# A convolution with fused attention and layer norm: the 7x7 convolution from two column tiles with 49 taps to four with 48 relative taps, and work moved between the engines

## What is computed

```python
k = conv(x, w1, dilation=2, padding=6) + b1
k = conv1x1(k, w2) + b2                       # 49 logits per pixel
attn = softmax(k, axis=1)
y = einsum('bkchw,bkhw->bchw', shifts(x), attn)
yc = states @ Cmat                            # states: scan s = A s + Bvec over the width
out = y + gelu(yc.T + y * D)
out = layernorm_over_channels(out) * ln_w + ln_b
```

## Time and profile before

| | us |
|---|---|
| median of 3 runs | 952.96 (952.06 to 953.69) |
| the profiled execution | 954.34 |
| its span | 952.2 |
| PE busy | 897.1, 94% |
| PEld busy | 762.8, 80% |
| DVE busy | 705.8, 74% |
| ACT busy | 418.9, 44% |
| POOL busy | 128.3, 13% |
| mean granted clock of PE | 0.977 |

### The profile page before, as it was taken

One profiled execution on the slowest core, in us unless ns is written; L12 is line 12 of the kernel. 1 busy time (PEld: TensorE's weight loads), 2 busy tenths in 40 slices (PEclk: granted clock), 3 DMA queues, 4 the chain that ended last, 5 costly groups with the idle time before them and its releaser, 6 DMA issues.

```text
span 952.2 us, 29640 instructions
## 1 busy us (share of the span) xinstructions
PE 897.1 (94%) x13764; PEld 762.8 (80%) x13764; DVE 705.8 (74%) x904; ACT 418.9 (44%) x499; POOL 128.3 (13%) x104
## 2 busy tenths in 40 slices
PE   4979889999999999999999999999999999999585
PEld 4979788877888788877888788878888788878572
DVE  0489957877878778877878877876978777875356
ACT  1134514435444544436444544435444543444436
POOL 1785000012100200012000200013000200012010
PEclk9979999999999999999999999999999999999779
DMA  9250050002340026002420027002520022002204
GB/s 299 63 89 3 1 91 2 3 1 46 64 73 3 1 46 134 3 1 45 85 53 2 1 46 135 2 2 45 104 34 2 2 47 45 2 2 46 45 2 88
DMA packets 133634, 41.92 MB, mean 44 GB/s; under 512 B 133175, under 2 KB 133256, under 8 KB 133256
## 3 DMA queue, kind: packets, MB, share of 16 engines
q1 hardware_dynamic: 132248, 40.01, 20.2%
q10 hardware_dynamic: 1264, 0.04, 0.1%
HBM read 23.27 MB, written 16.78 MB: 42 GB/s over the span
## 4 chain that ended last, share of the span: by engine, by line
PE 71%; DVE 10%; ACT 4%; issue 3%; DVEq 0%; ACTq 0%
PE cv L389 39%; PE wk L440 11%; PE wk L423 9%; PE wk L474 4%; PE ms L454 3%; PE ms L461 3%; DVE V L958 2%; ACT AT L660 2%; DVE o L1105 1%; DVE R L870 1%; PE ms L402 1%; ACT V L626 1%; DVE st L1046 1%; DVE chs L1048 1%; DVE st L1052 1%
## 5 line engine op out<-in xcount | busy, mean ns | idle before, releaser
L389 PE MATMUL cv<-V,W 128*49 128x248 f16 (+3 forms) x9408 | 545.0, 271 | 8.5 <-DVE V L958 4.3
L389 PEld LDWEIGHTS cv<-V,W 128*49 128x49 f16 x9408 | 478.1, 105 | 55.1 <-issue 34.7
L626 ACT ACTIVATE V<-R,sc 128x1024 f16<-128x1024 f32 (+1 forms) x88 | 110.7, 1261 | 23.0 <-DVE R L874 11.4
L958 DVE SCALAR_TENSOR_TENSOR V<-R,sc,V 128x1024 f16<-128x1024 f32 (+1 forms) x88 | 114.5, 1303 | 2.8 <-ACT V L626 1.8
L440 PE MATMUL wk<-band,XT 128*128 128x224 f16 (+1 forms) x960 | 110.2, 269 | 3.1 <-DVE o L1085 1.5
L440 PEld LDWEIGHTS wk<-band,XT 128*128 128x128 f16 x960 | 82.6, 99 | 31.3 <-issue 10.2
L267 POOL TENSOR_TENSOR chs<-o 128x1024 f32<-128x1024 f32 x14 | 33.0, 2355 | 497.3 <-DVE o L1085 471.5
L423 PEld LDWEIGHTS wk<-AT,sel 128*128 128x128 f16 x2560 | 80.5, 101 | 16.9 <-issue 10.9
L671 ACT ACTIVATE tg<-tg 128x1024 f32<-128x1024 f32 x32 | 33.8, 1058 | 132.5 <-DVE tg L1075 132.5
L423 PE MATMUL wk<-AT,sel 128*128 128x16 f16 x2560 | 88.8, 192 | 2.5 <-ACT AT L660 2.5
L1075 DVE SCALAR_TENSOR_TENSOR tg<-wk,sc,yc 128x512 f32<-128x512 f32 x64 | 47.7, 747 | 47.5 <-PE wk L440 47.5
(11 more groups left out here) (140 smaller groups left out, 785.7 us busy)
## 6 DMA issues: line engine op xcount, KB each, us to landing
raw<-in_x_dram SPq DMA_DIRECT2D x16, 1024.0 KB, 11.8
out_dram<-o SPq DMA_DIRECT2D x28, 512.0 KB, 4.9
w1raw<-in_L_conv_w_dram SPq DMA_DIRECT2D x2, 3136.0 KB, 17.7
out_dram<-o SPq DMA_DIRECT2D x8, 256.0 KB, 3.4
cm<-in_L_conv_Cmat_dram ACTq DMA_DIRECT2D x1, 32.0 KB, 8.8
dcol<-in_L_conv_D_dram ACTq DMA_DIRECT2D x2, 0.5 KB, 10.0
b2col<-in_L_conv_b_dram ACTq DMA_DIRECT2D x2, 0.2 KB
lnw<-in_L_conv_ln_w_dram ACTq DMA_DIRECT2D x2, 0.5 KB, 6.7
```

Source lines behind the costliest of these rows:

```text
L389: ins = pe.matmul(bank.rearrange("p (t c) -> p t c", c=COLS)[:, :, c0:c1], W[:, wl, h, s * K7 + v, :], V[a % RING][:, xl, w, t0:t0 + WIN, ...
L626: nc.scalar.activation(v_array(a, 0), array(a), ACT.Identity, scale=sc[:, par, 3:4]).then_inc(vhi, 1)
L958: nc.vector.scalar_tensor_tensor(out=v_flat(a, 1), in0=array_flat(a), scalar=sc[:, par, 3:4], in1=v_flat(a, 0), op0=ALU.mult, op1=ALU.subt ...
```

## The change

It keeps the algorithm and its units, and changes how the convolution is laid on PE and who does what.

- The 49th tap is subtracted from the weights of the others at the start (w2 relative to its last row, the bias too), and its logit is 0 (`last_tap`): 48 taps, kept as 32 and 16. `W` has the high and the low part side by side, 96 columns.
- A matmul has 32 or 16 weight columns on a column tile 32 wide (`tile_position`), and its data are both column parities at once (2 x 8 windows x up to 32 columns). Products run in 7 blocks of two (X and Y). Two (half, tap) steps of both are one double step of 20 matmuls, five per tile (`ROUNDS`): 49 double steps and 980 matmuls per unit for 1176.
- A sum is spread over partitions; some taps' parts lie on the fourth tile. ACT copies two of the sums (`sum_1`, `sum_2`), DVE adds the others straight from `cv` (`add_sum`, `fold_in`), now with both parities at once in four banks. `wk` goes from four banks to two; the logits are turned in two halves into it, and `gather_taps` adds the parts.
- The softmax: the shift is the exponential's bias and its sum comes out of `accum_out`, one instruction per 49 logits, 16 per unit.
- c0, c1, c2 and w are made by POOL (semaphore `pool_rows`). The bound on |x| is a sum of absolute values by ACT (`bound`) instead of DVE's maximum. ACT evacuates `apply`'s result (`attended`), and `gelu_args` and `residual` work on whole rows in SBUF.
- The second variance of unit m - 1, its inverse deviation and `normalise` move to the start of the next unit but one. `conv`'s first block of a unit waits for `logits_d` of the unit before it.

The lists of ACT and DVE after, for unit n (items of the next unit marked '):
ACT: v_high 2, 3; inverse_deviation(m-1,1); affines(m-1,1); exponentials 0-7; v_high 4; exponentials 8-15; v_high 5; attention_high; turned_attention; sum_1; band 0; v_high 6; band 1; v_high 7; bands 2, 3; bound' 0; bands 4, 5; bound' 1; band 6; v_high 8; bands 7, 8; v_high 9; band 9; sum_2; v_high 10; attended and gelu (0,0), (0,1), (1,0); v_high' 0; attended and gelu (1,1); squares 0; turned_x 0, 1; inverse_deviation 0; turned_x 2, 3; affines 0; turned_x 4, 5; squares 1; turned_x 6, 7; v_high' 1.
DVE: logits_i, logits_0 of m; v_low 2, 3; gather_taps 0; normalise(m-1,1); gather_taps 1; last_tap; softmax_shift; x2+, x2-; v_low 4; softmax_divide; v_low 5; attention_low; y2+, y2-; v_low 6; band 0; q2; band 1; v_low 7; band 2; q3; band 3; logits_1; band 4; q1; bands 5, 6; v_low 8; bands 7, 8; v_low 9; band 9; logits_2; u1', u0'; v_low 10; gelu_args (0,0); x1+'; residual (0,0); logits_rows; gelu_args (0,1); x1-'; residual (0,1); gelu_args (1,0); scales'; residual (1,0); v_low' 0; gelu_args (1,1); u2'; residual (1,1); centre 0; turned_x 0, 1; normalise 0; turned_x 2, 3; y1+'; turned_x 4, 5; y1-'; centre 1; turned_x 6, 7; v_low' 1; logits_d.

```diff
+REL = TAPS - 1
+TA, TB = 32, 16
...
+ROW_STEPS, POOL_ROWS = 17, 4
...
+M1P, M1M, M2P, M2M, M0, MD, MI = range(7)
+BLOCKS = (((M1P, 0, 0, 0), (M1M, 1, 1, 0)), ((M1P, 2, 2, 0), (M1M, 3, 3, 0)),
+          ((M2P, 4, 4, 0), (M2M, 5, 5, 0)), ((M2P, 6, 6, 0), (M2M, 7, 7, 0)),
+          ((M0, 8, 8, 0), (MD, 8, 9, 0)), ((M0, 9, 10, 1), (MI, 8, 11, 1)), ((M0, 9, 9, 0), (MI, 10, 12, 0)))
+NBLOCKS = len(BLOCKS)
+SUM_FIRST, SUM_LAST = (0, 0, 2, 2, 4, 4, 5), (1, 1, 3, 3, 6, 4, 6)
+BLOCK_ARRAYS = (2, 4, 6, 8, 9, 10, 11)
+BLOCK_SETS = (2, 4, 6, 8, 10, 12, 13)
...
+SLOT_FREE = (-3, -1, 0, 0, 1, 1, 2, 2, 3, 3, 4)
...
+STREAMS = {"A0": (0, 32, 0), "A1": (64, 96, 0), "A2": (0, 32, 1), "B0": (32, 64, 0), "B1": (32, 48, 1)}
...
+ROUNDS = ((X, 0, "A0", 0), (X, 1, "A1", 0), (X, 2, "B0", 0), (X, 3, "A2", 0),
+          (X, 0, "A0", 1), (X, 1, "A1", 1), (X, 2, "B1", 0), (X, 3, "A2", 1),
+          (Y, 0, "A0", 0), (Y, 1, "A1", 0), (X, 2, "B0", 1), (Y, 3, "B0", 0),
+          (Y, 0, "A2", 0), (Y, 1, "A0", 1), (X, 2, "B1", 1), (Y, 3, "B1", 0),
+          (Y, 0, "A1", 1), (Y, 1, "A2", 1), (Y, 2, "B0", 1), (Y, 3, "B1", 1))
...
-        cv = ctx.enter_context(nc.psum_tensor("cv", [P, 2, BANK], F32))
-        wk = ctx.enter_context(nc.psum_tensor("wk", [P, 4, BANK], F32))
+        cv = ctx.enter_context(nc.psum_tensor("cv", [P, 4, BANK], F32))
+        wk = ctx.enter_context(nc.psum_tensor("wk", [P, 2, BANK], F32))
...
+            def difference(buffer, par, j):
+
+                nc.gpsimd.tensor_tensor(R[buffer][:, :, :, :], rows_of(par, j + 2), rows_of(par, j),
+                                        ALU.subtract).then_inc(pool_rows, 1)
+
...
             def unit(n, par, nxt=True):
                 m = n - 1
-                sum_rows(m, 0)
+                make_c2(n, par)
+                make_w(n, par)
                 if nxt:
                     amax(n + 1, 1 - par)
+                    make_c1(n + 1, 1 - par)
+                sum_rows(m, 0)
                 sum_squares(m, 0)
                 sum_rows(m, 1)
                 sum_squares(m, 1)
-                pool.wait_ge(var_done, 2 * n)
+                if nxt:
+                    make_c0(n + 1, 1 - par)
...
+                for d in range(first, last):
+                    b, s = d // DSTEPS, 2 * (d % DSTEPS)
+                    if d % DSTEPS == 0:
+                        pe.wait_ge(vlo, ARRAYS * n + BLOCK_ARRAYS[b])
                         if cold:
+                            pe.wait_ge(w_low, 2 * BLOCK_SETS[b])
+                        if b == 0 and n:
+                            pe.wait_ge(z_step, ZSTEPS * n - 3)
+                        if b == 2 and n:
+                            pe.wait_ge(z_step, ZSTEPS * n)
+                        if b == 4:
+                            pe.wait_ge(z_step, ZSTEPS * n + 3)
+                        if b == 5:
+                            pe.wait_ge(z_step, ZSTEPS * n + 4)
+                    begun, left = set(), {(g, t): ROUNDS_LEFT[g, t] for g in (X, Y) for t in range(4)}
+                    for g, t, kind, later in ROUNDS:
+                        total, a, ws, t0 = BLOCKS[b][g]
+                        k0, k1, low = STREAMS[kind]
+                        h, v = (s + later) % HALVES, V_ORDER[(s + later) // HALVES]
+                        c0, c1 = max(0, PAD - v), min(COLS, COLS + PAD - v)
+                        left[g, t] -= 1
+                        to = cv[TILE * t:TILE * t + k1 - k0, bank_of(n)[total], :]
+                        ins = pe.matmul(to.rearrange("p (w t c) -> p w t c", w=2, c=COLS)[:, :, :, c0:c1],
+                                        W[:, ws, h * K7 + v, k0:k1],
+                                        slot(n, a)[:, low, :, t0:t0 + WIN, h, c0 + v - PAD:c1 + v - PAD],
+                                        skip_group_check=True, tile_position=(0, TILE * t),
+                                        start=(b == SUM_FIRST[total] and s == 0 and (g, t) not in begun),
+                                        stop=(b == SUM_LAST[total] and s == BLOCK_STEPS - 2 and not left[g, t]))
+                        begun.add((g, t))
...
+            def turn_logits(m, w):
+                if w == 0:
+                    pe.wait_ge(z_step, ZSTEPS * m + ZSTEPS)
+                    pe.wait_ge(xt_low, 8 * m + 8)
+                else:
+                    pe.wait_ge(soft, SOFT * m + 2)
+                for t in range(WIN):
+                    ins = pe.transpose(wk[:, t // 4, (t % 4) * P:(t % 4 + 1) * P],
+                                       Z[:, w, t].rearrange("p k c -> p (k c)"), id32[:, :])
+                ins.then_inc(lt_ready, 1)
...
-                if r >= 4:
-                    pe.wait_ge(blo, 10 * m + r - 3)
+                if r >= 2:
+                    pe.wait_ge(blo, 10 * m + r - 1)
...
-                if y >= 4:
-                    pe.wait_ge(o_made, 8 * m + y - 3)
+                if y >= 2:
+                    pe.wait_ge(xs_made, 8 * m + y - 1)
...
             def unit(n, par):
                 m = n - 1
+                conv(n, 0, 1)
+                if m:
+                    variance(m - 1, 1)
+                conv(n, 1, 3)
+                turn_logits(m, 0)
+                conv(n, 3, 5)
+                turn_logits(m, 1)
+                conv(n, 5, 16)
                 turn_attention(m, 0)
                 turn_attention(m, 1)
+                conv(n, 16, 18)
                 for r in range(BROWS):
                     spread(m, r)
+                    conv(n, 18 + r, 19 + r)
                 for y in range(8):
                     apply(m, y)
+                    conv(n, 28 + y, 29 + y)
+                    if y == 6:
                         mean(m, 0)
+                turn_x(n, par, 0)
+                conv(n, 36, 37)
+                turn_x(n, par, 1)
+                conv(n, 37, 39)
+                variance(m, 0)
+                conv(n, 39, 40)
+                for g in range(2, 6):
                     turn_x(n, par, g)
+                    conv(n, 38 + g, 39 + g)
                 mean(m, 1)
+                conv(n, 44, 45)
+                turn_x(n, par, 6)
+                conv(n, 45, 46)
+                turn_x(n, par, 7)
+                conv(n, 46, CONV)
...
+                nc.scalar.activation(tg[:].rearrange("p h r w -> p (h r w)"),
+                                     raw[par][:, h, PAD:PAD + ROWS, :].rearrange("p r w -> p (r w)"), ACT.Abs,
+                                     accum_out=amx[:, par, h:h + 1]).then_inc(amax_part, 1)
...
+            def exponentials(m, first, last):
+                act.wait_ge(soft, SOFT * m + 7)
+                for i in range(first, last):
+                    nc.scalar.activation(E[:, i, :], E[:, i, :], ACT.Exp, bias=st[:, 1, i:i + 1],
+                                         accum_out=st[:, 2, i:i + 1]).then_inc(exp_done, 1)
...
+            def attended(m, par, q, h):
+
+                if q == 0 and h == 0:
+                    act.wait_ge(o_free, 64 * m + 64)
+                for w in range(2):
+                    y = 4 * q + 2 * h + w
+                    act.wait_ge(y_done, 8 * m + y + 1)
+                    nc.scalar.activation(o[:, q, h, :, w:WIDTH:2], wk[:, y % 2, :].rearrange("p (r c) -> p r c", c=COLS),
+                                         ACT.Identity, scale=sc[:, par, applied_scale(m):applied_scale(m) + 1]
+                                         ).then_inc(xs_made, 1)
...
+            def add_sum(n, par, out, s, other, op, steps, p0=0, p1=P, scale=4):
+
+                dve.wait_ge(conv_done, NBLOCKS * n + SUM_LAST[s] + 1)
+                dve.wait_ge(z_step, ZSTEPS * n + steps)
+                nc.vector.scalar_tensor_tensor(out=out, in0=summed(n, s, p0, p1), scalar=sc[0:p1 - p0, par, scale:scale + 1],
+                                               in1=other, op0=ALU.mult, op1=op).then_inc(z_step, 1)
...
+            def gather_taps(m, w):
+
+                dve.wait_ge(lt_ready, 2 * m + w + 1)
+                dst = E[:, w * WIN:(w + 1) * WIN]
+                a = wk[:].rearrange("p b (t e k) -> p (b t) k e", e=P // TA, k=TA)[:, :, :, 0:2]
+                nc.vector.tensor_reduce(dst[:, :, 0:TA], a, AX, ALU.add).then_inc(soft, 1)
+                b = wk[:].rearrange("p b (t e k) -> p (b t) k e", e=P // TB, k=TB)[:, :, :, 4:8]
+                nc.vector.tensor_reduce(dst[:, :, TA:REL], b, AX, ALU.add).then_inc(soft, 1)
```

More of the change, by code:

```diff
@@ L733, in unit @@
                 affines(m, 0)
-                turned_x(n, par, (6, 8))
+                turned_x(n, par, 4, 6)
                 squares(m, 1)
-                products(n, par, 2)
-                inverse_deviation(m, 1)
+                turned_x(n, par, 6, 8)
                 if nxt:
-                    prepare(n + 1, 1 - par)
+                    v_high(n + 1, other, 1)
             def weights_high(first, last):
-                for h, s, src, scale, step in list(weight_parts())[HALVES * first:HALVES * last]:
+                for s in range(first, last):
```

(15 more changed lines are left out.)

901 lines of the change are left out of this document (443 added, 458 removed), and 3 rows, old and new, of the table PRODUCTS.

## The result

The changed kernel takes 978.62 us (median, 976.8 to 986.2) where the kernel before takes 953.17: 1.028 times as long by the means of the runs, 95% interval 1.023 to 1.034. I had said 945, range 925 to 972. The profiled execution took 977.36, with a span of 975.5; before it was 952.2, so 23.3 us are to be found.

A forecast was written before the change was run, and what follows sets the result against it. TensorE's own work was taken to bound units 1 to 7. From 954.3 us: seven units −11.2, unit 0 −4.5, tail +8.0, profiled launch to median −1.4, giving 945 us, range 925 to 972.

The forecast's parts named there:

- Unit 0: First unit: later convolution start, then turn_x(2) late behind VectorE's list; −4.5 us in all (−12 to +4).
- Rival C: Softmax exponentials slower: from 0.30 us each, the clock falls behind their wait too; 951 to 975 us, chance 0.38.
- e: Length of each of a unit's 16 small softmax exponentials on ScalarE: taken as 0.29 us, between 0.23 and 0.46.
- TensorE's work: TensorE's busy time per unit falls from 104.8 to 93.7 us, with convolution matmuls at 52 ns.
- Rival D: Convolution's four column tiles don't all run at once: 68 ns a matmul, 1015 to 1055 us, chance 0.08.
- Waits of a unit: TensorE's new waits in units 1 to 7, largest 4.7 at variance(m,0): together 9.2 us a unit.
- turn_x(4)'s 0.5: In each unit turn_x(4), with two banks, waits 0.5 us for normalise(m,0).
- Clock: TensorE's clock falls behind the variance wait, 1.6 us a unit; no charge at a unit's start.
- The port: GpSimd's six operations a unit hold VectorE steps with two SBUF inputs, mostly off the path; 0.2 us on it.
- Start 71.5: Unit 0's first convolution starts at 71.5 us for 67.04: x1_minus adds 1.2, low parts of two weight sets 3.
- turn_x(2) waits for VectorE's list: In unit 0 VectorE's list runs to 124 us; six turns and eleven double steps then give 142.
- Tail: After the last block: longer chain to turned attention +8.2, spreads +2, apply stage −2.3; together +8 us (+4 to +12).

The follow-up runs named there:

- e1: Changed kernel with VectorE's centring ahead of the last gelu_args and half of the squares ahead of the last gelu: 966.35 us.
- e2: Changed kernel with e1's order, variance later, array 1 and logits_d earlier at a unit's end, no work added or removed: 924.29 us.
- e3: Changed kernel with one exponential over the whole tile plus VectorE's subtraction and sum, in place of 16 exponentials: 971.54 us.
- e15: Changed kernel with only two waits added for GpSimd, so its difference c0 starts after VectorE's low parts: 979.25 us.
- e4b: Changed kernel with the four differences on VectorE instead of GpSimd: 986.49 us.
- e12: e2 with one exponential over the tile and array 5's low part ahead of the softmax's sum: 931.08 us.
- e13: e12 with GpSimd's difference w held until VectorE has made the attention's low part: 905.07 us.
- e5: Changed kernel with only unit 0's order altered: ScalarE's arrays 9, 10 and second sum ahead of two maxima, VectorE's turned x earlier: 972.65 us.

## Why the prediction was wrong

The median missed by 33.6 us, and the direction was wrong. Unit 0 missed by 12.5, the seven units by 15.7 together, the tail by 2.8; the rest, 2.7, is the step from the profiled launch to the median, which I had put at −1.4 and which was +1.3. The largest single step that failed is unit 0's; in the seven units it is several smaller ones.

Rival C (951 to 975) came nearest in time. Its condition was met, since e was 0.32 and C began at 0.30, but what it charged did not come: the wait was 2.4 and not 2.8, and the clock fell behind it in one unit of seven in the profile. So C is not what made the time.

- *TensorE's work:* said −11.1, measured −9.9. Bulk 52.4 ns for 52 adds 0.4 us; a piece of 20 takes 1.16 from start to start (1.13 to 1.20) against 20 × 52.4 = 1.05, so 0.11 a piece and not 0.09, 33 times: +0.7. Rival D is out: at 52.4 ns a matmul all four tiles run at once. The Trainium skill ("TensorE: Matmul & The Clock Gate", Part 3) gives 2.38 times for three column tiles, by my division 0.79 of full. Four tiles in this trace reach 50.5 of 52.4 ns, 0.96 of full, so that figure does not carry over.
- *Waits of a unit:* 9.2 said, 8.9 measured. The three large ones came within 0.3, and e1, e2 and e3 moved each at its place. The rest of the agreement is luck: turn_x(4)'s 0.5 did not come, and 0.68 at the first apply had no price.
- *Clock:* "I charge 1.6 behind the variance and none at a unit's start" was too small and too tidy. Behind the 4.4 us the seven units lost 1.7 to 2.9, 2.3 on the mean. Behind 2.3 to 2.5 us a unit lost nothing or about 1.6, which my rule from two idle times could not show. Work, waits and clock make 106.1 of 104.5 in a typical unit. Seven units came to +4.5 for −11.2: of these 15.7, 7 × 1.6 are this, about 3.5 the unit in which c0 came first, and some 1.6 the one in which double step 14 lost clock.
- *The port:* "c1 holds v_low(8) for 1.3 us" and the like walked the six operations once, at one set of times. It left out c0 at v_low(1) of the next unit, where one or the other is held from unit to unit, and the 3 us charged for the weights of unit 0 were too few: their second low part took 4.03 us where e15 has 1.68. On the whole the port cost the changed kernel little (e4b, e15), but 26 us as soon as the order was good (e12, e13).
- *Unit 0 is the largest step that failed,* 12.5 us. "Start 71.5" was 75.25; 2.1 of the difference is the held weights (e15), and the other 1.7 stays untraced. "turn_x(2) waits for VectorE's list ... to 124 ... 142": the list went to 133. Array 9 waited on ScalarE behind two maxima, which wait for the last weights. That gave TensorE the 5.65 us at 121.62 and pushed the rows, scales and turned x behind it (below, ScalarE of the changed kernel: a maximum, and array 9 behind both). I had summed VectorE's work and had not followed ScalarE's list. e5 shows it: 10.4 us by order alone.

```profile
113.73 1.91 ACT L738 ACTIVATE tg<-raw 128x2048 f32<-128x2048 f32 x1 [10.03 <-DVE W L1348]
...
117.74 1.30 ACT L713 ACTIVATE V<-R,sc 128x1152 f16<-128x1152 f32 x1
```

- *Tail:* +8 said, +10.8 measured. The turned attention is 15.8 us behind the turned logits for 8.5 before (+7.3). The spreads' two banks cost 2.5 (said: 2): with the 0.44 of wait between each pair they take 13.7 to the first apply, for 11.2. What failed is "The apply stage no longer waits for residuals: −2.3": from the first apply to the end it is 40.7 us for 39.8, +0.9.

## What to carry to other kernels

Where one engine fills a span and loses work, the gain is only there once every list that feeds it has been walked. Here the waits and the clock took back all ten microseconds a unit, and reordering the same work at a unit's end gave back 54 us in all. Walk the warm-up unit with all engines' lists, not with the busiest one's sum. Look for an operation of GpSimd that reads SBUF beside a VectorE step on which TensorE waits, and hold it until that step is issued: for w this was worth 26 us. Holding one that rarely meets such a step (c0 in e15) gave nothing that the runs can tell from no change.
